# Output projection split over the upper and lower 64 rows of the TensorE array, with the two halves added by VectorE

## What is computed

```
q, k, v = heads(x @ Wq + bq), heads(x @ Wk + bk), heads(x @ Wv + bv)
scores  = q @ k^T / sqrt(64) + where(adj, 0, -9e15)
ctx     = softmax(scores) @ v                 # back to (128, 128, 384)
y       = x + ctx @ Wf + bf
out     = (y - mean(y)) / sqrt(var(y) + 1e-5)  # over the 384 features
```

## Time and profile before

| | |
|---|---|
| median of three runs | 1020.2 us |
| the profiled execution, its own time | 1020.66 us |
| its span, first to last instruction | 1018.9 us |
| TensorE (PE) busy | 1003.8 us, 99% of the span, 7144 matmul records |
| VectorE (DVE) busy | 706.9 us, 69% |
| ScalarE (ACT) busy | 582.0 us, 57% |
| GpSimd (POOL) busy | 628.4 us, 62% |
| DMA | 179.64 MB, 176 GB/s on average |

### The profile page before, as it was taken

One profiled execution on the slowest core, in us unless ns is written; L12 is line 12 of the kernel. 1 busy time (PEld: TensorE's weight loads), 2 busy tenths in 40 slices (PEclk: granted clock), 3 DMA queues, 4 the chain that ended last, 5 costly groups with the idle time before them and its releaser, 6 DMA issues.

```text
span 1018.9 us, 26741 instructions
## 1 busy us (share of the span) xinstructions
PE 1003.8 (99%) x7144; PEld 902.7 (89%) x7144; DVE 706.9 (69%) x2832; ACT 582.0 (57%) x2117; POOL 628.4 (62%) x648
## 2 busy tenths in 40 slices
PE   9999999999999999999999999999999999999995
PEld 8888999888999888999889998889998899998894
DVE  4567766767766767767677667677667676676685
ACT  4666555665546664556655556645466645566550
POOL 1537766557765567665577565677655676655773
PEclk9999999999999999999999999999999999999998
DMA  8376676666676665766666766666666667664454
GB/s 205 80 193 183 179 196 189 185 176 170 182 188 180 174 183 173 197 166 182 188 176 169 195 180 179 171 175 188 186 174 176 184 174 200 167 181 157 136 176 140
DMA packets 340603, 179.64 MB, mean 176 GB/s; under 512 B 222688, under 2 KB 324192, under 8 KB 340576
## 3 DMA queue, kind: packets, MB, share of 16 engines
q1 hardware_dynamic: 339088, 178.35, 63.5%
q10 hardware_dynamic: 1488, 0.98, 0.3%
HBM read 103.75 MB, written 75.50 MB: 176 GB/s over the span
## 4 chain that ended last, share of the span: by engine, by line
PE 94%; DMA 2%; DVE 2%; ACT 1%; issue 1%; SPq 1%; POOLq 0%; POOL 0%; DVEq 0%; ACTq 0%
PE work_ps L403 20%; PE work_ps L404 19%; PE work_ps L405 19%; PE scores_ps L420 9%; PE scores_ps L434 8%; PE scores_ps L403 6%; PE scores_ps L404 6%; PE scores_ps L405 6%; DMA p_out<-p_turned 1%; ACT probs L811 1%; SPq L317 1%; DVE probs L615 1%; PE scores_ps L492 0%; DMA x_in<-in_x 0%; DVE stats L648 0%
## 5 line engine op out<-in xcount | busy, mean ns | idle before, releaser
L956 POOL TENSOR_TENSOR probs<-probs,inv_sum 128x768 f32<-128x768 f32 x128 | 188.6, 1473 | 329.8 <-DVE inv_sum L634 329.7
L811 ACT ACTIVATE probs<-probs,neg_max 128x128 f32<-128x128 f32 x768 | 298.6, 395 | 106.6 <-DVE neg_max L621 106.6
L615 DVE CUSTOM_DVE_ANT_0 probs<-scores_ps,mask_bias 128x128 f32<-128x128 f32 x768 | 172.1, 285 | 82.9 <-PE scores_ps L420 81.8
L951 POOL TENSOR_SCALAR y_sb<-y_sb,mean_var,rstd 128x384 f32<-128x384 f32 x122 | 202.0, 1656 | 21.9 <-POOL rstd L945 21.9
L820 ACT COPY v_sb<-work_ps 128x384 f32<-128x384 f32 x128 | 61.5, 481 | 213.1 <-PE work_ps L405 213.1
L811 ACT ACTIVATION_READ_ACCUMULATOR probs<-probs,neg_max 128x1 f32 x768 | 148.3, 193 | 0.0
L939 POOL TENSOR_TENSOR x_bias<-x_in,bias_row 128x384 f32<-128x384 f32 x128 | 127.4, 1017 | 9.1 <-DVE bias_row L774 9.1
L403 PE MATMUL scores_ps<-wf_hi,cT_hi 128*128 128x384 f32 x378 | 128.6, 340 | 0.0
L403 PE MATMUL work_ps<-wv_hi,xT_hi 128*128 128x384 f32 x381 | 127.9, 336 | 0.6 <-ACT qT L829 0.4
L404 PE MATMUL scores_ps<-wf_lo,cT_hi 128*128 128x384 f32 x378 | 128.2, 339 | 0.0
L405 PE MATMUL scores_ps<-wf_hi,cT_lo 128*128 128x384 f32 x378 | 128.2, 339 | 0.0
(11 more groups left out here) (80 smaller groups left out, 1887.2 us busy)
## 6 DMA issues: line engine op xcount, KB each, us to landing
p_out<-p_turned SPq DMA_DIRECT2D x128, 384.0 KB, 2.7
pT<-p_out SPq DMA_DIRECT2D x512, 96.0 KB, 2.2
x_in<-in_x SPq DMA_DIRECT2D x128, 192.0 KB, 2.9
out<-y_sb SPq DMA_DIRECT2D x124, 192.0 KB, 2.1
x_blocks<-in_x SPq DMA_DIRECT2D x360, 64.0 KB, 2.4
adj_u<-in_adj SPq DMA_DIRECT2D x32, 64.0 KB, 2.1
out<-xT SPq DMA_DIRECT2D x4, 192.0 KB, 1.9
pT<-in_L_gnn_Wf SPq DMA_DIRECT2D x1, 576.0 KB, 7.1
```

The source lines that it names most:

```text
L615: last = nc.vector.tensor_tensor_reduce(out=probs[:, e, h, :], in0=scores_ps[:, score_cols(e, h)], in1=mask_bias[:, e, :], scale=SCALE, sc ...
L811: last = nc.scalar.activation(probs[:, e, h, :], probs[:, e, h, :], ACT.Exp, bias=neg_max[:, e, h:h + 1], scale=1.0, accum_out=row_sum[:, ...
L951: nc.gpsimd.tensor_scalar(y_sb[:, e, :], y_sb[:, e, :], mean_var[:, at, 0:1], rstd[:, at, 0:1], ALU.subtract, ALU.mult).then_inc(y_ready, 1)
L956: nc.gpsimd.tensor_tensor(probs[:, e, :, :], probs[:, e, :, :], inv_sum[:, e, :].unsqueeze(2).broadcast_to([P, HEADS, SEQ]), ALU.mult).the ...
```

## The change

The four `out_product` of a step no longer use all 128 rows of the array. Each of the nine matmuls of a graph becomes two of 64 rows, one on the upper and one on the lower half, with two destinations: the bank of before and a second one (`SIDE_BANKS`, in `ending` `LAST_SIDE_BANKS`). Each bank then holds half of the sum over the features. VectorE adds the side bank to the residual (`y_half_added`), waits for that and adds the other bank (`y_added`). New waits on TensorE: `out_product` 0 waits for all four `mask_and_max` of the step (`max_found`), whose scores stood in the side banks; `out_product` 2 and 3 wait until the side bank of graph e-2 has been read; in group 31, `ctx_product` 0 and 1 wait for `y_half_added` of graphs 122 and 123, and each `out_product` for `y_added` of the graph four before.

```diff
+SIDE_BANKS = (2, 5, 2, 5)
+LAST_SIDE_BANKS = (0, 3, 1, 4)
...
+        def side_bank(e, n):
+
+            bank = LAST_SIDE_BANKS[e] if isinstance(n, int) and n >= LAST * GROUP else SIDE_BANKS[e]
+            return scores_ps[:, bank * BANK:bank * BANK + HID]
...
# ctx_product
-                if not isinstance(g, int) or g < LAST:
+                if isinstance(g, int) and g == LAST:
+                    if e < 2:
+                        past(pe, y_half_added, n - 2)
+                else:
                     past(pe, max_found, first_of(i, c) + GROUP + max(e, 1) - (e == 3))
...
# out_product
-                split_product(ctx_bank(e, n)[:, 0:HID], lambda k: (
-                    cT_hi[:, e, k, :], cT_lo[:, e, k, :], w_hi["f"][:, k, :], w_lo["f"][:, k, :]), out_done)
+                if isinstance(n, int) and n >= LAST * GROUP:
+                    past(pe, y_added, n - GROUP)
+                elif e == 0:
+                    past(pe, max_found, n + 2 * GROUP - 1)
+                if e >= 2:
+                    past(pe, y_half_added, n - 2)
+                dst = (ctx_bank(e, n)[:, 0:HID], side_bank(e, n))
+                for k in range(KC):
+                    for s, m in ((cT_hi, w_hi["f"]), (cT_hi, w_lo["f"]), (cT_lo, w_hi["f"])):
+                        for half in range(2):
+                            rows = slice(half * HEAD, (half + 1) * HEAD)
+                            last = nc.tensor.matmul(dst[half], s[rows, e, k, :], m[rows, k, :],
+                                                    start=k == 0 and s is cT_hi and m is w_hi["f"],
+                                                    stop=k == KC - 1 and s is cT_lo)
+                last.then_inc(out_done, 1)
...
# add_residual
-                nc.vector.tensor_tensor(y_slot(e, n), ctx_bank(e, n)[:, 0:HID],
-                                        x_bias[:, c % TURN * GROUP + e, :], ALU.add).then_inc(y_added, 1)
+                nc.vector.tensor_tensor(y_slot(e, n), side_bank(e, n), x_bias[:, c % TURN * GROUP + e, :], ALU.add
+                                        ).then_inc(y_half_added, 1)
+                dve.wait_ge(y_half_added, n + 1)
+                nc.vector.tensor_tensor(y_slot(e, n), ctx_bank(e, n)[:, 0:HID], y_slot(e, n), ALU.add
+                                        ).then_inc(y_added, 1)
```

More of the change, by code:

```diff
@@ L234, in attention_block @@
         y_added = sem("y_added")
+        y_half_added = sem("y_half_added")
         y_stats = sem("y_stats")
```

## The result

The changed kernel takes 1036.24 us (median of four runs, 1035.98 to 1036.83) against 1020.66 us for the kernel before in the same comparison: a ratio of 1.015, 95% interval 1.0137 to 1.0163. It is slower, where 1037.7 us had been forecast. The profiled execution has a span of 1034.1 us, 15.2 more than before.

What follows compares the result with a forecast made beforehand. TensorE, busy 99% of the span, was taken as the bound. Changes of form 13.0 + step 30 and ending 4.5 + 0 = 17.5 us on a span of 1018.9, so 1037.7 us on the median; 8 in 10 between 1022 and 1053.

Steps and rivals of the forecast that it cites:

- A pitch of 0.176 for the pair: Output products: a 64-row pair takes 0.176 us, as a full-array matmul does now, so the matmuls themselves bring nothing.
- (a): Rival, output products: the 64-row pair hides most of the exposed part, pitch 0.165, 11.9 us back, 1026 us; 22%.
- (b): Rival, output products: each matmul of a pair pays its own overhead, pitch 0.187, +11.9 us, 1049 us; 13%.
- (d): Rival, output products: float32r halves don't overlap, pitch 0.347, +185 us, 1205 us; 3%.
- Changes of form, 13.0 us: Both ends of a step's output products: 0.20 us going in (30 times), 0.24 coming out (29 times).
- Step 30 and the ending, 2.25 us each: Second additions 1, 2 and 3 lie on the chain in both places, +2.25 us each, together 4.5 us.
- The new waits cost nothing: TensorE's new waits on side banks and `max_found` cost nothing while VectorE reaches addition 0 before product 0 is done.
- Nothing in the steps from VectorE: Steps: VectorE's later additions, 2.25 us, are covered before scores and masks, with 0.6 us left before the masks; no cost.
- (e): Rival, steps: VectorE becomes late, masks start later each step, a microsecond more a step, 1060 to 1070 us; 3%.
- (c): Rival, faster: pair pitch falls to 0.162 and changes of form cost half, -4.1 us, 1016 us; 8%.

Runs made afterwards that it cites:

- the run with the halves in turn: Changed kernel with all nine upper-half matmuls of a graph, then all nine lower-half ones, instead of alternating: 1104.14 us (one run).
- the two half-and-half kernels: Changed kernel with main-bank addition only and pairs for two of four graphs, next to each other (0, 1) or apart (0, 2): 1030.49 and 1043.41 us.
- the two additions alone: Kernel before (128 rows, one bank), with VectorE adding twice, the second time the same bank again: 1025.32 us, ratio 1.004.
- runs of three: Changed kernel with three upper-half matmuls, then three lower-half ones, for each of three chunks: 1037.58 us, ratio 1.0166.
- The run with the output products beside the scores: Changed kernel with the four output products moved behind the four v products, right before the scores: 1189.65 us (one run).

## Why the prediction was right

The forecast was +17.5 us on the span; +15.2 was measured, 1036.24 us against 1037.7. The mechanism was right: the pairs bring nothing and the changes of form cost. The sizes of both costs were somewhat high, and the one for the ending came out near by luck.

- "A pitch of 0.176 for the pair": measured 0.176. The argument (float32r's extra goes with the type) is supported by the run with the halves in turn, where a single half has the same pitch. Each half pays its own overhead beside the other's, so neither (a) nor (b) holds, and (d) is out. The two matmuls of a pair start 3 to 5 ns apart, not 7. Why a float32r matmul takes some 0.013 us over its streaming, where float32 takes 2 or 3 ns (if its record streams the columns twice), stays open.
- Changes of form, 13.0 us: the mechanism held, shown by the two half-and-half kernels, the size was a little high. Measured 29 times 0.387 = 11.2 us, plus 0.18 in step 30. Going in was right (0.20). Coming out is 0.20, not 0.24: I had counted the slower third and fourth q matmuls of the earlier trace rows, which the v products hardly show (0.18). The plain start of the output products before, 0.24 and slightly slower first matmuls, fell away for another 0.01.
- Step 30 and the ending, 2.25 us each: the two places were right, each second addition is 0.6 us and not 0.75. In step 30 they cost 1.39 us, since VectorE's idle time takes in 0.39 of the 1.78. The ending grew by 2.15, but the additions behind the last ctx product are only 1.7 of it; a slower store added 1.1 and a faster last ctx product took 0.67 away, both of which the forecast did not have. "The new waits cost nothing" held in the steps; in the ending one of them is 0.9 us long, and no run shows what it costs there.
- Nothing in the steps from VectorE: right. The idle time before the masks was to be 0.6 us and is 1.2, mainly since the second addition is shorter. (e) is out: with the two additions alone the step is 30.97 us.
- (c), faster, would have needed a pair pitch near 0.160, the streaming alone; nothing came near it.
- Two slips in the sums change nothing. The time of (d), 1205 us, leaves the 17.5 us of the forecast out; with them it is 1223, as in the expectation of the run with the halves in turn. And 3 x 0.054 is 0.162 and not 0.160; with the 0.1734 us that its own division gives before rounding it is 0.161. One nanosecond there moves only (c) and its neighbours, by 1.1 us.

## What to carry to other kernels

Splitting a contraction of 128 into two halves that run side by side does the same work at the same pitch; it can win only what a pair saves over one matmul, and here, in float32r with 384 columns, that was nothing. Count the changes between full and 64-row products in TensorE's order first: 0.2 us going in and 0.2 coming out, per block and not per matmul, so gather such products in one block. Before moving a block to save a change, list what is queued on the other engines behind whoever waits for it.

## What was not expected of the hardware

TensorE's order is not strict between halves: with nine and nine, the lower half's first matmul started at 505.78 beside the upper half's sixth, ahead of three that stand before it, and with runs of three the overlap was complete (31.37 us against 31.36 a step). The same run splits the price of a change of form: at that seam, with no change of form, the newly used half's second matmul still comes 0.28 us after its first (505.78 to 506.06), the second of the two gaps. So 0.10 us of the 0.20 seems to be a first weight load with nothing to hide behind, and only the other 0.09 the change itself; no run separates them.

And a wait of 2.4 us of TensorE was once followed by a granted clock of 0.63 over the next 4.58 us, and once, at 2.3 us, it was not. The run with the output products beside the scores has 30 such waits, 29 of them 2.35 to 2.49 us long, and shows both outcomes. Here are 4.58 us from the start of the scores after two of its waits, each 2.40 us long:

```profile
122.34:126.92 4.58, 4.58 (x55) 4.18 (x56) 4.14 (x10) 0.00 (x0) 4.38 (x4) 1.00 0.24 91
158.78:163.36 4.58, 4.58 (x49) 4.46 (x49) 4.13 (x10) 0.00 (x0) 4.38 (x4) 0.63 0.30 107
```

After 12 of the 30 waits the clock stayed at 2.4 GHz and the scores took 2.95 us; after 18 of them part of the scores ran at 1.2 GHz (a mean of 0.63 to 0.68) and they took 4.2 to 4.6 us. So waits of the same length end either way, and what decides is not shown by any run.
